# Windowed-attention blocks on one core: tokens reordered so that one tile holds all padded-key work, xhat in two steps, constant rows by DMA

## The reference

```python
xn  = layer_norm(x) * w + b
xp  = pad(xn, to 28 x 28)                    # zeros after the norm
win = windows(xp, 14 x 14)                   # 4 windows per image, 196 tokens each
q, k, v = split(win @ qkv_w + qkv_b)         # 12 heads of 16 channels
attn = softmax(q @ k.T / 4 + rel_h[q row, k row] + rel_w[q col, k col])
x = x + unwindow(attn @ v) @ proj_w + proj_b # cut back to 16 x 16
x = x + gelu(layer_norm(x) @ fc1_w + fc1_b) @ fc2_w + fc2_b
```

## Time and profile before

| | us |
|---|---|
| median of 3 runs | 687.98 (686.68 to 695.04) |
| the profiled execution, its own time | 685.79 |
| its span, first to last instruction | 684.0 |
| mean granted PE clock | 0.885 of full |

### The profile page before, as it was taken

The page is one execution under the profiler, slowest core; times in us unless marked ns, Lnnn a source line. Parts: engine busy times, 40 slices in busy tenths (PEclk is TensorE's granted clock), DMA queues, the critical chain, the costliest instruction groups (busy, mean ns, idle before and its releaser), DMA issues.

```text
span 684.0 us, 12882 instructions
## 1 busy us (share of the span) xinstructions
PE 592.3 (87%) x4568; PEld 529.1 (77%) x4568; DVE 388.2 (57%) x930; ACT 309.3 (45%) x566; POOL 268.2 (39%) x470
## 2 busy tenths in 40 slices
PE   3588889898989898998998989898989898978766
PEld 2577777797979697987978878787879697967656
DVE  3415556658584847467364758567574847564221
ACT  1001052464637364543545555454646364637522
POOL 7333371616263444416135262526172534432100
PEclk9999585799998989798888999898989889999876
DMA  7421223121212222131121212121211222120000
GB/s 190 136 75 34 72 70 102 31 54 44 59 50 56 58 56 58 36 93 43 44 58 35 77 37 77 36 61 43 62 47 51 65 56 69 52 74 26 1 12 12
DMA packets 44079, 39.51 MB, mean 58 GB/s; under 512 B 6256, under 2 KB 42992, under 8 KB 44016
## 3 DMA queue, kind: packets, MB, share of 16 engines
q1 hardware_dynamic: 44016, 38.69, 21.1%
HBM read 6.82 MB, written 1.57 MB: 12 GB/s over the span
## 4 chain that ended last, share of the span: by engine, by line
PE 61%; issue 14%; DVE 11%; POOL 7%; ACT 3%; SPq 1%; DMA 1%; DVEq 0%; POOLq 0%; ACTq 0%
PE front L913 13%; PE back L834 11%; PE back L1072 8%; PE by_key L941 6%; PE by_query L971 5%; PE front L834 4%; POOL pad_e L424 4%; DVE xhat L665 3%; PE times_v L959 3%; PE front L929 2%; PE front L925 2%; POOL norm_rstd L392 2%; PE back L1052 2%; DVE att L753 1%; POOL pad_sum L462 1%
## 5 line engine op out<-in xcount | busy, mean ns | idle before, releaser
L771 DVE TENSOR_REDUCE row_max<-by_query 128x2 f32<-128x512 f32 x192 | 130.6, 682 | 48.8 <-PE by_query L971 48.5
L536 ACT ACTIVATE probs<-by_key 128x512 f32<-128x512 f32 x192 | 113.0, 593 | 92.6 <-PE by_key L941 92.2
L941 PE MATMUL by_key<-q_stack,k_stack 110*128 110x256 f32 x384 | 92.7, 339 | 1.6 <-ACT probs L536 1.2
L913 PEld LDWEIGHTS front<-q_t,rel_heads 96*84 96x84 f32 x896 | 91.1, 188 | 3.8 <-ACT rel_t L555 1.8
L913 PE MATMUL front<-q_t,rel_heads 96*84 96x32 f32 (+1 forms) x896 | 92.0, 272 | 2.1 <-ACT rel_t L555 1.1
L971 PE MATMUL by_query<-k_stack,q_stack 108*128 108x256 f32 x384 | 89.0, 326 | 2.5 <-DMA q_stack<-rel_lo 1.9
L941 PEld LDWEIGHTS by_key<-q_stack,k_stack 110*128 110x128 f32 x384 | 65.4, 216 | 17.3 <-issue 12.2
L971 PEld LDWEIGHTS by_query<-k_stack,q_stack 108*128 108x128 f32 x384 | 68.2, 221 | 3.6 <-DMA q_stack<-rel_lo 2.6
L1072 PE MATMUL back<-w,hid 128*128 128x192 f32 x384 | 69.8, 333 | 0.3 <-ACT hid L595 0.2
L834 PE MATMUL back<-xn_hi,w_hi 128*128 128x256 f32 x192 | 63.6, 338 | 2.7 <-DVE xn_hi L673 2.7
L1072 PEld LDWEIGHTS back<-w,hid 128*128 128x128 f32 x384 | 64.0, 196 | 1.0 <-ACT hid L595 0.7
(11 more groups left out here) (126 smaller groups left out, 1178.4 us busy)
## 6 DMA issues: line engine op xcount, KB each, us to landing
q_stack<-q_hi SPq DMA_DIRECT2D x64, 96.0 KB
k_stack<-k_hi SPq DMA_DIRECT2D x64, 96.0 KB
q_stack<-rel_hi SPq DMA_DIRECT2D x64, 84.0 KB
q_stack<-rel_lo SPq DMA_DIRECT2D x64, 84.0 KB
q_stack<-q_lo SPq DMA_DIRECT2D x32, 96.0 KB
k_stack<-k_lo SPq DMA_DIRECT2D x32, 96.0 KB
out<-X SPq DMA_DIRECT2D x8, 192.0 KB, 2.2
X<-in_x SPq DMA_DIRECT2D x1, 1344.0 KB, 9.2
```

Source lines behind the costliest of these rows:

```text
L536: act.activation(probs[h % NP][:, :, :], KB[h % 2][:, :].rearrange("p (k t) -> p k t", k=2), ACT.Exp).then_inc(s_ex, 1)
L771: dve.tensor_reduce(row_max[:, h, :], QB[h % 2][:, :].rearrange("p (a t) -> p a t", a=TILES), AX, ALU.max).then_inc(s_smax, 1)
L913: last = pe.matmul(dst[:, :, at, :], rel_heads[L][:, w, WS - 1 - i:2 * WS - 1 - i, :] .rearrange("p k h -> p (k h)"), grid[:, :, at, :], s ...
L941: last = pe.matmul(KB[h % 2][:, c * TOK:(c + 1) * TOK], k_stack[par][0:ROWS, h, c * P:(c + 1) * P], q_stack[par][0:ROWS, h, :], start=True ...
```

## The change

The host sends each image's tokens in another order: first the 224 tokens of columns 0 to 13, row by row, then the 32 of columns 14 and 15. The large window is then tokens 0 to 195, and tile 0 lies wholly in it. The host puts the output back in order. Then:

- rel_tok and all padded-key steps are made for the second tile alone; pad_top, pad_sum and pad_out of tile 0 are set once, to NEG and zeros.
- by_key gives the first key tile 196 query columns (fp32r) and the second 256: 452 in all; the exponential and times_v follow. by_query is as before.
- rel0 and rel1 need the 16x16 grid: ACT copies q_t to q_grid in two instructions, and rel_t is written in two instructions (columns 0 to 13, columns 14 and 15) on ACT and on DVE.
- Norms: DVE subtracts the mean from both tiles in one instruction right after the variance, and multiplies both by the root in one when POOL has made it; eps is added from a tile.
- Setup: POOL only rounds the two constant tiles; SP copies the constant rows of the stacks from there by DMA, each row repeated for 12 heads. X's remainder is issued after the first stack's. The qkv bias product of layer 0 goes to bank VB behind the first transposes; ACT and DVE do the first norm's parts ahead of the weights; setup_vectors comes after k. columns[0] is loaded ahead of the qkv weights; the first by_query waits for the constants instead of SP.

The core of the diff (many waits are only recounted for one tile and are left out):

```diff
 PE_AT: -bias1=-51, ..., rel_tok0=-11, rel_tok1=-8     +bias0=-42, bias1=-51, ..., rel_tok=-11
 ACT_AT: -weights1=-51, rel_tok1=-1                    +weights1=-45, q_grid=-36, rel_tok=-1
 DVE_AT: -weights1=-47, rel_tok0=-13                   +weights1=-45, bias0=-43, setup=-31
 POOL_AT: -stacks=-45                                  +norm_b=-45
+INNER = WS * WS
+TALL = SIDE * WS
+KEYS = INNER + TOK
-NEG = -1.0e30
+NEG = -2.0 ** 100
...
-        rel_tok = sb("rel_tok", [P, TILES, RW])
+        rel_tok = sb("rel_tok", [P, RW])
-        probs = [sb(f"probs{i}", [P, 2, TOK]) for i in range(NP)]
+        probs = [sb(f"probs{i}", [P, KEYS]) for i in range(NP)]
+        q_grid = sb("q_grid", [GF, 2, TOK])
+        rows_rounded = xn_hi[1]
...
+        def tall(t):
+            return t[:, :, 0:TALL].rearrange("p g (r c) -> p g r c", c=WS)
+        def edge(t):
+            return t[:, :, TALL:TOK].rearrange("p g (r c) -> p g r c", c=EDGE)
...
+            for par in range(2):
+                sp.wait_ge(s_rounded, 1)
+                for stack, lo, hi, c in ((q_stack, R_MASK, R_MAX, 1), (k_stack, R_RHI, ROWS, 0)):
+                    sp.dma_start(stack[par][lo:hi, :, :].bitcast(F32),
+                                 rows_rounded[lo:hi, c:c + 1, :].bitcast(F32).broadcast_to([hi - lo, HEADS, TOK])
+                                 ).then_inc(s_stack0[par], 16)
+                if par == 0:
+                    sp.dma_start(X[:, TILES:, :], x_t[:, TILES:, :]).then_inc(s_x, 16)
-            sp.dma_start(X[:, TILES:, :], x_t[:, TILES:, :]).then_inc(s_x, 16)
...
-            def constant_rows(par):
-                pool.wait_ge(s_const, C_LOADS)
-                pool.tensor_copy(q_stack[par][:, :, :],
-                                 query_rows.unsqueeze(1).broadcast_to([P, HEADS, TOK])).then_inc(s_stack0, 1)
-                pool.tensor_copy(k_stack[par][:, :, :],
-                                 key_rows.unsqueeze(1).broadcast_to([P, HEADS, TOK])).then_inc(s_stack0, 1)
+            def round_rows():
+                pool.wait_ge(s_rows, 32)
+                pool.tensor_copy(rows_rounded[:, :, :], hid[:, 0:2, :]).then_inc(s_rounded, 1)
...
-                    for a in range(TILES):
-                        src = rel_tok[:, a, 0:2 * HEADS * WS].rearrange("p (h k) -> p h k", k=WS)
+                    src = rel_tok[:, 0:2 * HEADS * WS].rearrange("p (h k) -> p h k", k=WS)
...
-                    act.activation(probs[h % NP][:, :, :], KB[h % 2][:, :].rearrange("p (k t) -> p k t", k=2),
-                                   ACT.Exp).then_inc(s_ex, 1)
+                    act.activation(probs[h % NP][:, :], KB[h % 2][:, 0:KEYS], ACT.Exp).then_inc(s_ex, 1)
...
+                if t == ACT_AT["q_grid"]:
+                    act.wait_ge(s_qto, n + 1)
+                    act.wait_ge(s_rel, 2 * n)
+                    grid = q_grid[:, :, :].rearrange("p g (r c) -> p g r c", c=SIDE)
+                    act.activation(grid[:, :, :, 0:WS], tall(q_t), ACT.Copy)
+                    act.activation(grid[:, :, :, WS:SIDE], edge(q_t), ACT.Copy).then_inc(s_qg, 1)
...
-                    act.activation(rel_t[:, 0, :, :], FB[0:GR, :].rearrange("p (g t) -> p g t", g=2),
-                                   ACT.Copy).then_inc(s_relo, 1)
+                    out, src = rel_t[:, 0, :, :], FB[0:GR, :].rearrange("p (g r c) -> p g r c", g=2, c=SIDE)
+                    act.activation(tall(out), src[:, :, :, 0:WS], ACT.Copy)
+                    act.activation(edge(out), src[:, :, :, WS:SIDE], ACT.Copy).then_inc(s_relo, 1)
...
-                dve.tensor_scalar(norm_var[i][:, :], norm_mv[i][:, :, 1], EPS[L], None, ALU.add).then_inc(n_var[i], 1)
+                dve.tensor_tensor(norm_var[i][:, :], norm_mv[i][:, :, 1], eps[L][:, :], ALU.add).then_inc(n_var[i], 1)
+                dve.wait_ge(n_tr[i], n)
+                dve.tensor_tensor(xhat[i][:, :, :], xs, norm_mv[i][:, :, 0:1].broadcast_to([P, TILES, D]),
+                                  ALU.subtract).then_inc(n_sub[i], 1)
-                for a in range(TILES):
-                    last = dve.scalar_tensor_tensor(xhat[i][:, a, :], xs[:, a, :], norm_mv[i][:, a, 0:1],
-                                                    norm_rstd[i][:, a:a + 1].broadcast_to([P, D]),
-                                                    ALU.subtract, ALU.mult)
-                last.then_inc(n_hat[i], 1)
+                dve.wait_ge(n_sub[i], n + 1)
+                dve.tensor_tensor(xhat[i][:, :, :], xhat[i][:, :, :],
+                                  norm_rstd[i][:, :].unsqueeze(2).broadcast_to([P, TILES, D]),
+                                  ALU.mult).then_inc(n_hat[i], 1)
...
-                if t == DVE_AT["rel_tok0"]:
-                    dve.tensor_copy(rel_tok[:, 0, 0:4 * GR].rearrange("p (x h k) -> p x h k", h=GH, k=WS),
-                                    FB[:, 0:4 * GR].rearrange("p (x k h) -> p x h k", h=GH, k=WS))
-                    dve.tensor_copy(rel_tok[:, 0, 4 * GR:RW], FB[:, 4 * GR:RW]).then_inc(s_rto, 1)
...
-                if t in (PE_AT["rel_tok0"], PE_AT["rel_tok1"]):
+                if t == PE_AT["rel_tok"]:
+                    pe.wait_ge(s_relo, 2 * (n + 1))
                     for w in range(2):
                         for g in range(2):
                             col = (w * 2 + g) * GR
-                            pe.transpose(FB[:, col:col + GR], rel_t[:, w, g, a * P:(a + 1) * P],
-                                         ident[0:GR, 0:GR])
+                            pe.transpose(FB[:, col:col + GR], rel_t[:, w, g, P:TOK], ident[0:GR, 0:GR])
...
-                    for c in range(2):
-                        last = pe.matmul(KB[h % 2][:, c * TOK:(c + 1) * TOK],
-                                         k_stack[par][0:ROWS, h, c * P:(c + 1) * P],
-                                         q_stack[par][0:ROWS, h, :], start=True, stop=True)
+                    for c, (lo, hi) in enumerate(((0, INNER), (INNER, KEYS))):
+                        last = pe.matmul(KB[h % 2][:, lo:hi], k_stack[par][0:ROWS, h, c * P:(c + 1) * P],
+                                         q_stack[par][0:ROWS, h, 0:hi - lo], start=True, stop=True)
...
-                    for c in range(2):
+                    for c, (lo, hi) in ((1, (INNER, KEYS)), (0, (0, INNER))):
                         for i in range(QUAD):
                             h = g * QUAD + i
-                            last = pe.matmul(VB[i * VW:(i + 1) * VW, 0:TOK], v_ones[n % NV][:, c, h, :],
-                                             probs[h % NP][:, c, :], start=(c == 0), stop=(c == 1))
+                            last = pe.matmul(VB[i * VW:(i + 1) * VW, 0:hi - lo], v_ones[n % NV][:, c, h, :],
+                                             probs[h % NP][:, lo:hi], start=(c == 1), stop=(c == 0))
...
+    rows, cols = np.divmod(np.arange(TOK), SIDE)
+    order = np.concatenate([np.flatnonzero(cols < WS), np.flatnonzero(cols >= WS)])
+    x = dram("in_x", np.asarray(inputs["x"]).reshape(IMAGES, TOK, D)[:, order])
```

More of the change, by code:

```diff
@@ L54 @@
 NSEG = 3
-NEG = -1.0e30
+NEG = -2.0 ** 100
 SETUP_DVE = 2 * 2
-ZEROED = 4 + 2 * NV
+ZEROED = 7 + 2 * NV
 COLS = 4 + 4 + MC + 4
-C_LOADS = 16 * 4
+C_LOADS = 16 * 2
 V_LOADS = 16 * 2 * 2
@@ L101, in build @@
         ident = sb("ident", [P, P])
-        pad_mask = sb("pad_mask", [P, NSEG, TILES * HEADS])
+        pad_mask = sb("pad_mask", [P, NSEG, HEADS])
         head_mask = sb("head_mask", [GF, GH])
         minus_half = sb("minus_half", [P, TILES])
+        eps = [sb(f"eps{L}", [P, TILES]) for L in range(2)]
         w1_in = sb("weights_in", [P, 2, MLP])
@@ L151, in build @@
         v_ones = [sb(f"v_ones{i}", [P, TILES, HEADS, VW]) for i in range(NV)]
[L152 to L158, removed]
+        pad_e = sb("pad_e", [P, 2 * HEADS, WS])
+        seg_max = [sb(f"seg_max{i}", [P, 2, HEADS]) for i in range(2)]
+        seg_sum = [sb(f"seg_sum{i}", [P, 2, HEADS]) for i in range(2)]
+        pad_max = sb("pad_max", [P, NSEG, HEADS])
+        pad_prod = sb("pad_prod", [P, NSEG, HEADS])
+        pad_top = sb("pad_top", [P, TILES, HEADS])
+        pad_w = sb("pad_w", [P, NSEG, HEADS])
         row_max = sb("row_max", [P, HEADS, TILES])
@@ L211, in build @@
         n_var = [sem(f"norm{i}_var") for i in range(2)]
+        n_sub = [sem(f"norm{i}_centred") for i in range(2)]
         n_rstd = [sem(f"norm{i}_rstd") for i in range(2)]
@@ L369, in _ @@
         def _(pool):
+            for L in range(2):
+                pool.memset(eps[L][:, :], EPS[L]).then_inc(s_eps, 1)
+            pool.memset(minus_half[:, :], -0.5).then_inc(s_zero, 1)
             pool.memset(wqkv_hi[:, :, QKV:WCOLS].bitcast(F32), 0.0).then_inc(s_zero, 1)
@@ L406, in biases_and_pads @@
             def biases_and_pads(n, L, par, t):
-                if t == POOL_AT["stacks"] and n == 0:
+                if t == POOL_AT["norm_b"] and n == 0:
+                    round_rows()
                     widen_norm_b()
-                    for i in range(2):
```

(15 more changed lines are left out.)

207 lines of the change are left out of this document (100 added, 107 removed).

## The result

The changed kernel takes 666.75 us (median of 4 runs, 662.08 to 671.54), the kernel before 690.93 on the same chip (4 runs, 686.68 to 695.04): a ratio of 0.9651, with a 95% interval of 0.9552 to 0.975. The forecast was 664, with a range of 630 to 696.

What follows compares the result with a forecast made beforehand. PE's own work was taken to bound one part of each image, the DVE the other. Span 684.0 + 20 (start) - 31 (images) - 9 (clock) - 1.5 (last image) = 662.5, plus 1.8: 664.3, forecast 664, range 630 to 696.

Steps and rivals of the forecast that it cites:

- The two parts: Each image: PE bounds from norm-2 transposes to next q product, DVE from there to next transposes; gains 1.0 and 1.2 us.
- (a): PE's part: relative positions go to token layout for one tile, not two, saving 0.67 us per image.
- (b): PE's part: first key tile meets 196 queries, not 256, in by_key; gain 0.2 us per image.
- (c): PE's part: one quad of times_v goes from 512 columns to 452; gain 0.1 us per image.
- (d): DVE's part: seg_max works on one tile instead of two, ending 0.32 us earlier per image.
- (e): DVE's part: xhat's subtraction runs beside POOL's root, leaving one multiplication behind it; gain 0.9 us per image.
- rival 3: xhat's multiplication waits for q_lo too, so its gain and the clock's are gone: 686 us, chance 0.10.
- (f): PE's clock: a shorter idle stretch before norm 2's transposes means less half clock; 0.7 us per image, 9 over 13.
- rival 4: The clock doesn't fall any more after PE's idle stretch: 35 us lower, 629 us, chance 0.08.
- The start: Setup before by_query of image 0: two 62-partition stack transfers on two DMA engines make it 20 us later.
- rival 2: The stack transfers use all DMA engines, so the start is 8 us earlier: 636 us, chance 0.15.
- fourteen images' worth: Repeated stretch: 13 images and the half-filled ends each gain 2.2 us, 31 us in all.

Runs made afterwards that it cites:

- e10: Changed kernel with key rows in two transfers, k_lo waiting for xhat, and tile 1's relative-position token layout made twice: 0.70 us more distance, 12 us more in the median.
- e3: Changed kernel with xhat in its old form, two instructions behind the root and no subtraction ahead: 700.01 us, ratio 1.0202.
- e4: Changed kernel with POOL's k_lo waiting until xhat's multiplication of norm 2 is done: 627.30 us, ratio 0.9137.
- e7: Kernel before the change, with only k_lo's wait for xhat of norm 2 added: 624.73 us, ratio 0.9107.
- e5: Changed kernel with the token layout of tile 1's relative positions made twice on PE, same results: 670.51 us, ratio 0.9685.
- e9: Changed kernel with key rows in two transfers, k_lo waiting for xhat, and 256 queries for both key tiles (512 columns): median within the range of e6.
- e6: Changed kernel with key rows in two transfers (48 and 14 partitions) and k_lo waiting for xhat's multiplication: 600.43 us, ratio 0.8757.
- e0: The changed kernel run again unaltered, for the spread: 668.78 us, ratio 0.9717.
- e1: Changed kernel with each stack's key rows in two transfers, of 48 and 14 partitions, instead of one of 62: 634.01 us, ratio 0.9257.

## Why the prediction was right, step by step

**The bound.** As read from the earlier trace rows: e10 shows PE's part to bound (0.67 of work put in, 0.70 of distance out), e3, e4 and e7 show the stretch up to xhat to bound. The two parts gained 0.84 and 1.19 where 1.0 and 1.2 were forecast. By the prediction's own signs it holds: the twelve distances are 34.9 in the mean (34.7 forecast, wrong if over 36), and by_query of image 0 comes at 77.65 (74, wrong if before 55).

**(a), rel_tok.** 0.67 forecast, 0.70 measured in e5 and e10, by a second copy of tile 1's group in place of tile 0's.

**(b), by_key.** The direction was right, but 0.2 was too much. Of by_key only the double group shortens in the chain, 0.06 at full clock; with (c)'s 0.10 that is the 0.17 between e9 and e6. I had scaled every head by its columns, and the single pairs didn't move at all. What a single pair waits for is open; no run was made for it.

**(c), times_v.** 0.1 forecast, 0.10 measured.

**(d), seg_max.** 0.32 forecast. Not run alone, but e3 has all of the change except xhat's new form, and its DVE part is 0.31 shorter than before's (12.86 for 13.17). The DVE's rows between q_t and norm_var last as before but for seg_max, 0.55 instead of 0.90.

**(e), xhat.** 0.9 forecast; 0.92 by the idle time and 0.88 by e3. The mechanism came as worked out: the multiplication started as k_lo did, ended 0.4 after it (1.60 us, as forecast), and did not wait for q_lo, so rival 3 falls. The subtraction delays the root by 0.25 us; I had allowed up to 0.4.

The Trainium skill, SBUF — State Buffer, section SBUF: two separate sides, says that a DVE instruction with two SBUF inputs and a GpSimd instruction that reads SBUF share one pair of ports, and that whichever starts first keeps it for its whole instruction. The traces agree in both directions, to within 0.2 us: the multiplication lasts 1.60 beside k_lo, ending 0.40 after it, and 0.56 without it; the root lasts 0.95 beside the subtraction, ending 0.56 after it, and 0.70 without it.

**(f), the clock.** 0.7 per image forecast, 0.8 measured. That is luck: 0.7 was a guess between 0 and 3.4, and the same kernel's clock gives 0.8 by one execution and 0.5 by another (e0). The runs now give the points, of one execution each, less the 0.1 to 0.2 that the eighth distance adds to a mean: PE idle 2.6 to 2.7 us before the transposes costs 3.0 (before) to 3.9 us a distance (e3); 1.8 us costs 2.2 (after), 2.5 (e0) or 1.5 (e1); and 0.7 costs nothing (e4, e6) to 0.6 (e7). The clock's part of e4 was larger than the idle time itself, and of e3 as well. That the same edit brings 1.05 us of distance and some 2 of clock was the largest thing that the prediction put too low: it stood as rival 4 with 0.08, without the edit that makes it come true.

**The start.** +20 forecast. by_query of image 0 came at 77.65, not 74 (+24). POOL's first bias at 64.33, where about 61 was forecast, is near it by luck: two sizes were off and nearly cancel. The stacks' rows took some 16 us each at 42 to 47 GB/s, not 24 at the 32 of the earlier trace rows's smaller transfer, so 15 us less; but the loads that were to run beside them, for 4 us more, ran between and behind them, some 22 us (26 to 34 and 50 to 64), since SP was held in issuing. Of the 24 us, 6 were won again before the first norm-2 transposes, so +18.1. e1 shows that the width was the cause; rival 2 would have been right with another cut of the same rows. The rule of the Trainium skill that the prediction cites (DMA: Bandwidth & Descriptors, section Why a DMA increments its semaphore by 16 and not by 1), that a transfer uses the largest number of engines up to 16 that divides its slowest dimension, agrees: 62 partitions show a DMA share of 0.14 (two of 16 would be 0.125), 48 and 14 show 0.94.

**The sum.** The twelve distances gave 35.2 where 12 x 2.9 = 34.8 was forecast, the pair at the layer change among them (86.70 to 79.85, 6.9 for two). The part that failed is the ends: "fourteen images' worth", the clock's thirteenth and the last image came to 41.5 - 34.8 = 6.7 us behind the twelfth distance, and 2.1 were measured. The thirteenth distance gained 2.5 (31.80 to 29.29), but the two of the half-filled end nothing (26.0 and 28.19 before, 26.54 and 27.97 after), nor did the last image alone, for which I had 1.5. Why the end doesn't gain wasn't tried. The start's 1.9 us less and the ends' 4.6 us more nearly cancel, and with the twelve distances' 0.4 the span came to 664.8 instead of 662.5. That the total is so close is luck in two places: these two cancel, and the twelve distances of e0, the same kernel, gained 28.9 and not 35.2.

## What to carry to other kernels

Where an engine's last instruction ahead of a hand-over shares its port with another engine, look at what that other engine starts just then, and hold it back: on the kernel before one wait, 0.9 us for POOL, saved 2.0 us of every image, and the clock 2.4 more (mean distance 36.73 to 32.32), so a stall of 2 us is worth taking apart even where PE is busy 87% of the span. And before a large load is put on a queue, factor its partition count: 62 partitions at once held up everything behind them for some 15 us apiece, 48 and 14 for under 5 us (3.07 and 4.79, the longest issues of e1's start).

## What the runs showed that I had not expected

- From image to image the stretches at half clock last 3.4, 6.8 or 10.2 us (17.1 at the start and the end of the changed kernel), each 3.4 us costing a distance 1.55. So the same kernel gives 31.57, 33.1, 34.65 or 36.26 us for the same image's work, and no single distance or median is fit to judge an edit of 0.2 us.
- The issue of a transfer behind a slow one can hold SP for 15 us (14.94 and 15.12; the second q_stack transfer 8.41), though an issue is 0.4 to 0.9 us for most others.
- A pair of by_key between other work takes 0.23 to 0.24 us at 512, 452 and 384 columns per head, while a double group falls by 0.06 for each 60 columns per head. What the single pair waits for is open.
- The exponentials have 60 columns fewer (543 ns instead of 593 each), and it doesn't show in the distance: ACT isn't the bound here, but for the 1.19 us of the eighth distance, which are there at either width (32.35 in e9, 32.17 in e6, each 1.65 above its distance).
